# A fused four-layer model on one core: the third expert layer's order, VectorE splits, and a hand-written order in the last layer

## The chip, the cores and the metric

The kernel runs on one core of a Trainium2 chip. The metric is the device time of one execution in microseconds (us); the time before is the median of three runs. TensorE (PE in the profile) multiplies, VectorE (DVE), ScalarE (ACT) and GpSimd (POOL) do the element-wise work, and SyncE (SP) issues transfers.

## The reference, cut to what matters

Activations `x` of 4 batches x 512 tokens x 256 numbers go through eight steps, an attention and an expert layer in turn, each added to its input after a layer norm. All is float32.

```
x = x + L0_xattn(norm(x), ctx);  x = x + L0_ffn(norm(x))
x = x + L1_xattn(norm(x), ctx);  x = x + L1_ffn(norm(x))
x = x + L2_xattn(norm(x), ctx);  x = x + L2_ffn(norm(x))
x = x + L3_xattn(norm(x), ctx);  x = x + L3_ffn(norm(x))
```

The change touches three expert layers:

```
L0_ffn:  gates = softmax(x @ Wg); top 2, made to sum to 1
         out = sum over 8 experts e of weight[e] * (x @ We[e] + be[e])
L2_ffn:  shared = swiglu(x @ w_shared_in) @ w_shared_out
         hid = swiglu(x @ w1_shared)          # swiglu(a, b) = silu(a) * b
         out = shared + sum over 8 experts e of weight[e] * (hid @ w2[e])
L3_ffn:  scores = (relu(x @ W1 + b1) @ W2 + b2) * sigmoid(tanh(x @ Wg1 + bg1) @ Wg2 + bg2)
         e = argmax(softmax(scores));  out = x * scale[e] + bias[e]
```

## The kernel before, in words

The program is eight phases, numbered 0 to 7: attention in the even ones, experts in 1, 3, 5 and 7. Tokens are worked on in 4 batches of 4 tiles of 128. Every phase has one list of steps, `self.order`, and every engine walks that same list in order and issues its own part of each step. So a step's place in the list sets its place in the queue of every engine at once. In most phases the list comes from places on a number line: `spread(steps, begin, end)` gives steps evenly spaced places, and `in_order` sorts by them; a batch `g` has its main work at places `g` to `g + 1`. Within a step, semaphores order the engines. The results of TensorE go to the 8 PSUM banks in turn (`Ring`); a step that uses a bank waits until its last user has been emptied (`drained`). At a phase's start VectorE, ScalarE and GpSimd wait until all engines have left the phase before (`wait_left`); TensorE does not.

**Splits.** Products in phases 1, 3 and 5 need more precision than one pass gives: an operand is kept as `hi` (a rounded copy, made by ScalarE) and `lo` (the rest, a subtraction), and `mm3` multiplies hi by hi, hi by lo and lo by hi. In phases 1 and 5 the `lo` of the normed activations is made by GpSimd (`RowPairs.gpsimd`, L1205 to L1209), and the `lo` of the weights half by GpSimd, half by VectorE (`split_lo`, L1329 and L2334).

**Third expert layer** (`FeedForward2`, phase 5). A batch's first layer, the steps `f2_hidden`, multiplies 512 tokens by the two input weights in 4 steps of 12 matmuls of 512 columns. A step's two banks go through ScalarE (`silu`, L2324), VectorE (product, L2366), ScalarE (`hidden_hi`, L2329) and GpSimd (`hidden_lo`, L2409). Then each tile has one `f2_shared` step (6 matmuls of 256 columns; it waits for the last `hidden_lo`) and 4 `f2_routed` steps (6 of 512 each), which VectorE adds to `x` weighted (L2373, L2383). All 4 hidden steps stand at the head of the batch's list, in front of its own first tile.

**Last expert layer** (`FeedForward3`, phase 7). Batch 0 is worked on inside phase 6; 1 to 3 are left, and batch 3 has its layer norm still to come. Per batch: `f3_hidden` (two, relu and tanh), `f3_scores`, `f3_rows` (normed rows), `g_exp`, `g_div`, `g_top`, `g_places` (softmax and argmax on VectorE, `g_exp` on ScalarE), `f3_hot` (one-hot), `f3_turn` (transposed), and 4 `f3_row` (the chosen scale and bias rows by a matmul, times and plus on VectorE, the last sum on GpSimd). A batch is stored by one transfer when its four tiles are done.

Of the kernel before, what the change touches and what calls it, by code (L numbers as in the profile page):

```python
# [16 lines left out]
P = 128  # L17
# [5 lines left out]
KC = DM // P  # L23
# [204 lines left out]


def hT_read(c, f, b):  # L230

    def visited(step):
        k, v = c.at(step)
        return c.filled(k), v
    if f in (0, 4, 6):
        return [visited(("query", f, b, 1))]
    if f in (1, 5):
        return [visited(("logits", f, b)), (c.sem("h_lo"), c.nth["h_split", f, b])]
# [950 lines left out]
class RowPairs:  # L1189
# [14 lines left out]

    def gpsimd(self, e, step):  # L1205
        c, g = self.c, step[2]
        e.wait_ge(c.sem("h_hi"), c.nth[step])
        e.tensor_tensor(self[g].lo[:, :, :], c.hT[:, :, rows_of(g)], self[g].hi.bitcast(F32)[:, :, :],
                        ALU.subtract).then_inc(c.sem("h_lo"), 1)  # L1209

    def wait_made(self, e, g):
        e.wait_ge(self.c.sem("h_lo"), self.c.nth["h_split", self.f, g])


class FeedForward0:
# [53 lines left out]
    def tensor(self, e):  # L1269
        c, f, gates = self.c, self.f, self.gates  # L1270
        for step in self.order:
# [7 lines left out]
            elif kind == "f0_experts":  # L1279
# [5 lines left out]
                if t == 0:  # L1285
                    e.wait_ge(c.sem("f0_we_lo_pool"), e2 + 1)
                    e.wait_ge(c.sem("f0_we_lo_dve"), e2 + 1)
                if v > 1:
# [39 lines left out]

    def split_lo(self, e, k, sem):  # L1329

        c = self.c
        for e2 in range(E0 // 2):
            es = slice(2 * e2, 2 * e2 + 2)
            e.wait_ge(c.sem("f0_we_hi"), 2 * e2 + k + 1)
            e.tensor_tensor(self.we.lo[:, k, es, :], self.we_in[:, k, es, :], self.we.hi[:, k, es, :].bitcast(F32),  # L1335
                            ALU.subtract).then_inc(sem, 1)

    def vector(self, e):
        c, f, gates, norm = self.c, self.f, self.gates, self.norm
        for step in self.order:  # L1340
            kind = step[0]
            if kind == "f0_we":
                self.split_lo(e, 1, c.sem("f0_we_lo_dve"))
            elif kind == "logits":
# [47 lines left out]
    def gpsimd(self, e):  # L1392
        self.gates.make_iota(e)
        for step in self.order:
            if step[0] == "f0_we":
                self.split_lo(e, 0, self.c.sem("f0_we_lo_pool"))
            elif step[0] == "h_split":
                self.h.gpsimd(e, step)
            else:
                self.norm.gpsimd(e, step)  # L1400
# [785 lines left out]
class FeedForward2:  # L2186
# [28 lines left out]
    def work(self, sc, mine):  # L2215
# [8 lines left out]


        self.parts = [(name, k, slice(None)) for name in ("wsi", "w1", "wso") for k in range(KC)]
# [4 lines left out]
        for g in range(BATCH):  # L2231
# [20 lines left out]
    def wait_pair(self, e, name, e2=0):  # L2252

        c, n = self.c, {"wsi": 1, "w1": 2, "wso": 3, "w2": 4 + e2}[name]
        e.wait_ge(c.sem("f2_lo_pool"), n)
        e.wait_ge(c.sem("f2_lo_dve"), n)

# [75 lines left out]

    def split_lo(self, e, share, k, sem):  # L2334

        for n in self.shares[share]:
            name, q, part = self.parts[n]
            if q == k:
                e.wait_ge(self.c.sem("f2_hi"), n + 1)
                pair = self.pairs[name]  # L2340
                e.tensor_tensor(pair.lo[:, q, part], self.w[name][:, q, part], pair.hi[:, q, part].bitcast(F32),
                                ALU.subtract).then_inc(sem, 1)
# [53 lines left out]
    def gpsimd(self, e):  # L2396
        c, f = self.c, self.f
        self.gates.make_iota(e)
        for step in self.order:
            kind = step[0]  # L2400
            if kind == "f2_split":
                self.split_lo(e, step[2], 0, c.sem("f2_lo_pool"))
            elif kind == "h_split":
                self.h.gpsimd(e, step)
            elif kind == "f2_hidden":
# [12 lines left out]
class FeedForward3:  # L2418
# [76 lines left out]
    def work(self, sc, mine):  # L2495
# [170 lines left out]
class Phases:  # L2666
# [76 lines left out]
    def sync(self, e):  # L2743
        c = self.c
        for chain in CHAINS:
# [10 lines left out]
            for f in chain:  # L2756
                if f == 2:
                    self.wait_left(e, f)
                self.all[f].sync(e)
        for b in range(BATCH):  # L2760
            e.wait_ge(*x_final(c, LAST_PHASE, b))
            e.dma_start(c.out[b].rearrange("(t p) d -> p t d", p=P), c.x[:, 4 * b:4 * b + 4, :]).then_inc(c.sem(f"store{b}"), 16)
        for b in range(BATCH):
            e.wait_ge(c.sem(f"store{b}"), 16)

# [83 lines left out]
```

## Time and profile before

| what | value |
|---|---|
| median of 3 runs | 2894.68 us (2892.67 to 2896.89) |
| the profiled execution's own time | 2907.88 us |
| its span, first to last instruction | 2906.1 us |
| mean granted TensorE clock | 0.939 of full |
| TensorE busy | 2738.4 us, 94% |
| VectorE busy | 1632.2 us, 56% |
| ScalarE busy | 1579.1 us, 54% |
| GpSimd busy | 310.1 us, 11% |

Times in the trace are counted from the start of the span. Phase 1 begins at about 770 us, phase 5 at 1890 and phase 7 at 2853. In a row of the timeline the brackets say how long the engine had been idle before it and who released it. "PEclk" is the share of the full TensorE clock that was granted in a stretch: 1.00 is 2.4 GHz, 0.50 is 1.2 GHz. A busy TensorE that runs at 0.50 still counts as busy.

### The profile page before, as it was taken

To read this page: it belongs to the slowest core of one execution; us is meant where nothing else is said; L and a number is where in the kernel's file an instruction comes from. 1 tells how busy PE (TensorE), PEld (TensorE's weight loads), DVE (VectorE), ACT (ScalarE), POOL (GpSimd) and SP (SyncE) were. 2 spreads that over 40 slices of the span, in tenths; PEclk is the share of its full clock that TensorE was granted. 3 is DMA by queue.
4 is the path that set the end of the run, shared out by engine and by line. 5 is a ranking of instruction groups with operands and counts; after the bars stand their busy time and mean duration, and the time that the engine had idled before them with its cause. 6 is when DMAs were issued, how large, how long until landed. Compare 5 with 4: busy or idle time off the path is not lost.

```text
span 2906.1 us, 38394 instructions
## 1 busy us (share of the span) xinstructions
PE 2738.4 (94%) x14432; PEld 1356.7 (47%) x14432; DVE 1632.2 (56%) x2990; ACT 1579.1 (54%) x2687; POOL 310.1 (11%) x259
## 2 busy tenths in 40 slices
PE   7999999999899889999899999989999999999986
PEld 3334444343475557776333333368643443434333
DVE  6777777777375554442112221057576777777834
ACT  2777777777501112111687878831247777777762
POOL 2010100100111001211001010031301010010001
PEclk7899999999899999999999999989979998999977
DMA  5332243331200001001744545110133423324200
GB/s 120 62 45 42 40 53 51 46 34 13 88 1 29 1 15 51 1 1 43 108 56 68 76 56 62 44 48 1 29 47 50 57 47 46 56 32 50 24 1 29
DMA packets 68588, 125.13 MB, mean 43 GB/s; under 512 B 20963, under 2 KB 45102, under 8 KB 64950
## 3 DMA queue, kind: packets, MB, share of 16 engines
q1 hardware_dynamic: 67254, 120.25, 27.0%
q10 hardware_dynamic: 1152, 2.44, 0.3%
q8 instruction: 116, 1.90, 0.3%
q14 instruction: 66, 0.54, 0.1%
HBM read 42.11 MB, written 2.10 MB: 15 GB/s over the span
## 4 chain that ended last, share of the span: by engine, by line
PE 82%; DVE 9%; ACT 4%; issue 3%; SPq 2%; POOL 0%; DMA 0%; ACTq 0%; POOLq 0%; DVEq 0%
PE psum L190 53%; PE psum L726 19%; PE psum L1977 6%; DVE mpart L916 4%; ACT probs L794 3%; SPq L1032 1%; PE psum L279 1%; PE psum L736 1%; PE psum L1970 0%; SPq L1033 0%; DVE stats L306 0%; PE psum L745 0%; DVE parts L1798 0%; DVE hrow L331 0%; DVE we_pair_lo L1335 0%
## 5 line engine op out<-in xcount | busy, mean ns | idle before, releaser
L794 ACT ACTIVATE probs<-psum 128x512 f32<-128x512 f32 (+3 forms) x2080 | 1279.5, 693 | 403.2 <-PE psum L190 401.3
L916 DVE TENSOR_REDUCE mpart<-psum 128x2 f32<-128x804 f32 x1024 | 977.0, 991 | 323.1 <-PE psum L190 314.8
L726 PE MATMUL psum<-probs,vt 128*17 128x512 f32 (+1 forms) x4992 | 675.9, 617 | 1.4 <-ACT probs L794 1.4
L190 PE MATMUL psum<-qst,kst 50*128 50x512 f32 (+3 forms) x2496 | 615.0, 458 | 16.6 <-ACT probs L794 5.5
L190 PEld LDWEIGHTS psum<-qst,kst 50*128 50x128 f32 (+3 forms) x2496 | 273.6, 188 | 428.9 <-issue 270.0
L190 PE MATMUL psum<-kst,qst 48*128 48x402 f32 x2048 | 419.3, 435 | 39.3 <-DVE mpart L916 37.1
L190 PEld LDWEIGHTS psum<-kst,qst 48*128 48x128 f32 x2048 | 203.1, 201 | 347.9 <-issue 183.8
L190 PE MATMUL psum<-wv,ctxT 128*128 128x256 f32 (+1 forms) x624 | 185.3, 424 | 1.1 <-DVE vt L906 0.5
L726 PEld LDWEIGHTS psum<-probs,vt 128*17 128x17 f32 (+1 forms) x4992 | 85.0, 96 | 201.8 <-issue 161.3
L190 PE MATMUL psum<-ctxT,wk 128*128 128x512 f32 (+1 forms) x384 | 157.9, 541 | 9.5 <-DMA ctxT<-in_ctxT 8.0
L190 PEld LDWEIGHTS psum<-wv,ctxT 128*128 128x128 f32 (+1 forms) x624 | 110.2, 196 | 78.9 <-issue 59.9
L2022 ACT ACTIVATE inner<-psum 128x512 f32<-128x512 f32 x32 | 19.1, 597 | 214.6 <-PE psum L1977 214.6
L342 POOL TENSOR_TENSOR rstd<-veps,half 128x4 f32<-128x4 f32 x32 | 34.3, 1072 | 830.9 <-DVE veps L311 830.9
L989 POOL TENSOR_TENSOR kp_lo<-kp_lo,kp_hi 128x512 fp32r<-128x512 f32 x80 | 83.1, 1042 | 271.4 <-ACT kp_hi L783 205.1
L190 PEld LDWEIGHTS psum<-ctxT,wk 128*128 128x128 f32 x384 | 64.2, 193 | 89.9 <-issue 73.0
L906 DVE COPY vt<-psum 128x256 f32<-128x256 f32 (+1 forms) x52 | 22.1, 424 | 146.1 <-PE psum L190 146.1
L190 PE MATMUL psum<-we_pair_hi,masked_lo 128*128 128x512 f32 x256 | 88.1, 412 | 4.0 <-POOL we_pair_lo L1335 4.0
L1977 PE MATMUL psum<-masked_hi,w_hi 128*128 128x512 f32 x224 | 91.7, 409 | 0.0
L1977 PE MATMUL psum<-masked_hi,w_lo 128*128 128x512 f32 x224 | 89.4, 399 | 0.0
L1977 PE MATMUL psum<-masked_lo,w_hi 128*128 128x512 f32 x224 | 89.0, 397 | 0.0
L293 ACT ACTIVATE hT<-psum 128x512 f32<-128x512 f32 x56 | 32.9, 601 | 84.5 <-PE psum L279 84.4
L817 ACT ACTIVATE vt<-psum 128x256 f32<-128x256 f32 (+1 forms) x104 | 40.0, 392 | 63.9 <-PE psum L190 58.9
(325 smaller groups left out, 2710.7 us busy)
## 6 DMA issues: line engine op xcount, KB each, us to landing
kst<-kp_hi SPq DMA_DIRECT2D x144, 200.1 KB, 5.9
ctxT<-in_ctxT SPq DMA_DIRECT2D x36, 512.0 KB, 5.2
kst<-kp_lo SPq DMA_DIRECT2D x72, 200.1 KB, 5.4
qst<-qp_hi SPq DMA_DIRECT2D x144, 64.0 KB, 4.5
kst<-kp_hi SPq DMA_DIRECT2D x84, 100.1 KB, 2.9
qst<-qp_lo SPq DMA_DIRECT2D x72, 64.0 KB, 5.1
kst<-kp_lo SPq DMA_DIRECT2D x42, 100.1 KB, 3.0
stage<-in_L_ffn_W SPq DMA_DIRECT2D x16, 256.0 KB, 4.4
```

Of the source, the lines that this page charges most:

```text
L190: last = e.matmul(dst, lhsT, rhs, start=i == 0, stop=i == len(pairs) - 1)
L279: t = e.transpose(c.bank(k)[:, at:at + P], h[:, q * P:(q + 1) * P], c.ident[:, :])
L293: e.activation(dst, src, ACT.Copy).then_inc(c.drained(k), 1)
L342: e.tensor_tensor(c.rstd[:, ts], c.veps[:, ts], c.half[:, :], ALU.pow).then_inc(c.sem("rsqrt_made"), 1)
L726: t = e.matmul(c.bank(self.acc)[32 * h:32 * h + VW, :], self.vt[0:kn, kc, self.head(g, h), :], p[0:kn, h % self.wide, :], start=kc == 0, s ...
L736: t = e.transpose(bank[:, at], self.accs[:, at], c.ident[:, :])
L794: e.activation(self.probs[n % slots][0:kn, :, :], c.psum[0:kn, k:k + self.wide, :], ACT.Exp if softmax else ACT.Sigmoid, scale=DH ** -0.5) ...
L817: e.activation(dst, src, ACT.Copy).then_inc(c.drained(k), 1)
L916: e.tensor_reduce(self.mpart[:, :, p * (SEQ // P) + qt, i], c.psum[:, k:k + 2, 0:MAX_WIDTH], AX.X, ALU.max).then_inc(c.drained(k), 1)
L989: e.tensor_tensor(raw.bitcast(F32R), raw, hi.bitcast(F32), ALU.subtract).then_inc(c.sem("parts_made"), 1)
L1032: e.dma_start(ks.bitcast(F32)[rows, halves, :], k.bitcast(F32)[head, halves, :]).then_inc(sem, 16)
L1977: t = e.matmul(bank, *pair, start=i > 0 and j == 0, stop=j == len(passes) - 1)
```

## The change

1. **Splits.** The `lo` of the weights in phases 1 and 5, and of batch 0's activations in both, is made by VectorE alone. GpSimd keeps the activations of batches 1 to 3. Two semaphores of halves (`..._pool`, `..._dve`) become one.
2. **Third expert layer.** The 4 hidden steps of batches 1, 2 and 3 get the places `g - 0.26` to `g - 0.25`, inside the batch before them; batch 0's take 0 to 0.25 and its tiles 0.25 to 1.
3. **Last expert layer.** The order is written out. The last batch's norm comes early, and the adding of rows late.
4. **Last store.** Batch 3 is stored by two transfers of two tiles.

```diff
-    def gpsimd(self, e, step):
+    def low(self, e, step):
         c, g = self.c, step[2]
         e.wait_ge(c.sem("h_hi"), c.nth[step])
         e.tensor_tensor(self[g].lo[:, :, :], c.hT[:, :, rows_of(g)], self[g].hi.bitcast(F32)[:, :, :],
-                        ALU.subtract).then_inc(c.sem("h_lo"), 1)
+                        ALU.subtract).then_inc(low_rows_made(c, self.f, g)[0], 1)
...
             if kind == "f2_split":
-                self.split_lo(e, step[2], 1, c.sem("f2_lo_dve"))
+                self.split_lo(e, step[2])
+            elif kind == "h_split" and step[2] == 0:
+                self.h.low(e, step)
...
-            main = [("f2_hidden", f, g, which, i) for which in range(2) for i in range(KC)]
+            hidden = [("f2_hidden", f, g, which, i) for which in range(2) for i in range(KC)]
+            placed += spread(hidden, 0, 0.25) if g == 0 else spread(hidden, g - 0.26, g - 0.25)
+            main = []
...
-            placed += spread(ready, g - 0.9, g - 0.15) + spread(main, g, g + 1)
+            placed += spread(ready, g - 0.9, g - 0.15) + spread(main, g if g else 0.25, g + 1)
...
-        self.order = in_order(spread(self.batch_steps(1), -0.4, 0.15) + spread(self.norm.steps(f, 3), 0, 0.35)
-                              + spread(self.batch_steps(2), -0.1, 0.45) + spread(self.batch_steps(3), 0.37, 1))
+        self.order = hidden(1) + norm[:5] + hidden(2)[:1] + scores(1) + hidden(2)[1:] + norm[5:8] + rows(1) + norm[8:]
+        self.order += places(1) + scores(2) + hidden(3)[:1] + rows(2) + [("f3_turn", f, 1)] + hidden(3)[1:] + places(2)
+        self.order += [("f3_rows", f, 3)] + added(1) + scores(3) + [("g_exp", f, 3), ("f3_turn", f, 2)] + places(3) + added(2)
+        self.order += [("f3_turn", f, 3)] + added(3)
...
+            dst, size = c.out[b].rearrange("(t p) d -> p t d", p=P), 4 if b + 1 < BATCH else 2
+            for t in range(0, 4, size):
+                e.wait_ge(c.sem("f3_added"), c.nth["f3_row", LAST_PHASE, 4 * b + t + size - 1])
+                e.dma_start(dst[:, t:t + size, :], c.x[:, 4 * b + t:4 * b + t + size, :]).then_inc(c.sem(f"store{b}"), 16)
```

Here `places(g)` is `g_div`, `g_top`, `g_places`, `f3_hot`; `rows(g)` is `f3_rows`, `g_exp`; `added(g)` the four `f3_row`; and `norm` the last batch's norm without its idle place.

The first place is VectorE's queue at the start of phase 5, before (the `x` row is phase 4's last work, `w_202` is the routed part's input weight):

```order
L968 TENSOR_TENSOR x<-x,psum 128x256 x4
L2355 TENSOR_TENSOR gate_v<-psum,gb 128x32
L2341 TENSOR_TENSOR wsi_pair_lo<-wsi,wsi_pair_hi 128x512
L2341 TENSOR_TENSOR w_pair_lo<-w_202,w_pair_hi 128x512
L1121 TENSOR_REDUCE gate_m<-gate_v 128x4
```

and now:

```order
L975 TENSOR_TENSOR x<-x,psum 128x256 x4
L1216 TENSOR_TENSOR hpair_lo<-hT,hpair_hi 128x1024
L2364 TENSOR_TENSOR gate_v<-psum,gb 128x32
L2348 TENSOR_TENSOR wsi_pair_lo<-wsi,wsi_pair_hi 128x512 x2
L2348 TENSOR_TENSOR w_pair_lo<-w_202,w_pair_hi 128x512 x2
```

VectorE has gained the activations' `lo` and the second halves of both weights; GpSimd has lost them. Phase 1 begins in the same way.

The second place is VectorE's queue where batch 0 of phase 5 ends and batch 1 begins, before:

```order
L2373 TENSOR_TENSOR x<-x,psum 128x256
L2383 SCALAR_TENSOR_TENSOR x<-psum,gate_v,x 128x256 x8
L2366 TENSOR_TENSOR silu<-silu,psum 128x512 x3
L306 BN_STATS stats<-x 128x6
L308 BN_AGGR meanvar<-stats 128x2
L2366 TENSOR_TENSOR silu<-silu,psum 128x512
L2373 TENSOR_TENSOR x<-x,psum 128x256
```

and now:

```order
L2392 SCALAR_TENSOR_TENSOR x<-psum,gate_v,x 128x256 x4
L1155 TENSOR_TENSOR gate_hot<-iota,gate_idxf 128x32 x2
L2375 TENSOR_TENSOR silu<-silu,psum 128x512 x4
L2392 SCALAR_TENSOR_TENSOR x<-psum,gate_v,x 128x256 x4
L1167 TENSOR_TENSOR gate_hot<-gate_hot,gate_top_241 128x32 x2
L1169 TENSOR_TENSOR gate_v<-gate_hot 128x32
L2382 TENSOR_TENSOR x<-x,psum 128x256
L2392 SCALAR_TENSOR_TENSOR x<-psum,gate_v,x 128x256 x8
```

The four products of batch 1 (`silu`) now stand in the middle of batch 0's third tile, with half of that tile and the whole fourth behind them. Batches 2 and 3 have theirs in front of the fourth tile of the batch before. TensorE's queue is in the same order.

The third place is TensorE's queue in the last layer, before (`relu` and `tanh` mark the scores, `hrow` the last batch's norm, `hot` the transposed one-hot rows):

```order
L190 MATMUL psum<-hT,wg_218 128x512 x2
L190 MATMUL psum<-w_219,relu 128x16 x4
L2551 MATMUL psum<-ident,hot 48x128 x4
L190 MATMUL psum<-wg_220,tanh 128x1 x4
L190 MATMUL psum<-scale_bias,hotT 128x512 x4
L2551 MATMUL psum<-ident,hot 48x128 x4
L279 MATMUL psum<-ident,hrow 128x128 x8
L190 MATMUL psum<-scale_bias,hotT 128x512 x2
L190 MATMUL psum<-hT,w_217 128x512 x2
```

and now:

```order
L190 MATMUL psum<-hT,wg_218 128x512 x2
L286 MATMUL psum<-ident,hrow 128x128 x8
L190 MATMUL psum<-w_219,relu 128x16 x4
L190 MATMUL psum<-wg_220,tanh 128x1 x4
L190 MATMUL psum<-hT,w_217 128x512 x2
L2558 MATMUL psum<-ident,hot 48x128 x4
L190 MATMUL psum<-hT,wg_218 128x512 x2
L190 MATMUL psum<-scale_bias,hotT 128x512 x4
```

The norm's transposes, and with them batch 3's hidden steps, stand in front of all rows of scales and biases.

## Rows read from the trace of the kernel before

**Rows 1.** The page: its first line, and the chain that ended last, by engine

```profile
span 2906.1 us, 38394 instructions
...
PE 82%; DVE 9%; ACT 4%; issue 3%; SPq 2%; POOL 0%; DMA 0%; ACTq 0%; POOLq 0%; DVEq 0%
```

**Rows 2.** Timeline of TensorE, phase 5: start, us, engine, line, instruction, idle before

```profile
1895.61 0.76 PE L190 MATMUL psum<-hpair_hi,wsi_pair_hi 128*128 128x512 f32 x1 [3.82 <-POOL wsi_pair_lo L2341]
...
1915.21 0.55 PE L190 MATMUL psum<-wso_pair_hi,hidden_hi 128*128 128x256 f32 x1 [6.33 <-issue]
...
1916.63 3.42 PE L190 MATMUL psum<-wg,hT 128*128 128x8 f32 x16
...
1960.69 0.36 PE L190 MATMUL psum<-wso_pair_hi,hidden_hi 128*128 128x256 f32 x1 [3.73 <-issue]
...
2005.41 0.36 PE L190 MATMUL psum<-wso_pair_hi,hidden_hi 128*128 128x256 f32 x1 [2.96 <-issue]
...
2049.48 0.36 PE L190 MATMUL psum<-wso_pair_hi,hidden_hi 128*128 128x256 f32 x1 [2.96 <-issue]
```

**Rows 3.** Stretches of phase 5: length; PE, PEld, DVE, ACT, POOL busy; PEclk, DMA

```profile
1915.00:1924.00 9.00, 8.79 (x32) 7.95 (x33) 1.67 (x5) 0.34 (x1) 2.57 (x3) 0.50 0.00 0
1925.00:1946.00 21.00, 21.00 (x103) 17.68 (x102) 16.66 (x54) 0.23 (x1) 0.00 (x0) 1.00 0.00 1
1946.00:1960.00 14.00, 10.96 (x49) 8.75 (x47) 4.24 (x8) 8.20 (x11) 6.79 (x5) 1.00 0.00 1
1960.00:1972.00 12.00, 11.30 (x47) 9.90 (x48) 4.52 (x14) 0.23 (x1) 0.59 (x1) 0.72 0.00 0
2004.00:2012.00 8.00, 6.59 (x25) 5.47 (x26) 4.06 (x13) 0.00 (x0) 2.12 (x2) 0.79 0.01 3
```

**Rows 4.** Timeline of VectorE, GpSimd and TensorE at the start of phase 1

```profile
772.11 7.56 DVE L1335 TENSOR_TENSOR we_pair_lo<-we,we_pair_hi 128x512 fp32r<-128x512 f32 x4
...
774.03 6.78 POOL L1335 TENSOR_TENSOR we_pair_lo<-we,we_pair_hi 128x512 fp32r<-128x512 f32 x4
...
775.85 0.77 PE L190 MATMUL psum<-we_pair_hi,masked_lo 128*128 128x512 f32 x1 [3.98 <-POOL we_pair_lo L1335]
```

**Rows 5.** Timeline of VectorE, phase 5: a split while GpSimd is idle

```profile
1923.83 0.68 DVE L2341 TENSOR_TENSOR w_pair_lo<-w,w_pair_hi 128x512 fp32r<-128x512 f32 x1
```

**Rows 6.** Instructions of the tile hpair_lo: durations in ns, least, median, most

```profile
L2072 DVE TENSOR_TENSOR masked_lo<-hpair_lo,psum x16: 1210/1211/1215, 1087.6 to 1290.8; 128x1024 fp32r<-128x1024 f32 x16
```

**Rows 7.** Timeline of GpSimd and ScalarE, batch 0 of phase 5

```profile
1891.34 2.35 POOL L1208 TENSOR_TENSOR hpair_lo<-hT,hpair_hi 128x1024 fp32r<-128x1024 f32 x1 [0.50 <-ACT hpair_hi L1203]
...
1913.41 1.70 POOL L2409 TENSOR_TENSOR hidden_lo<-silu,hidden_hi 128x512 fp32r<-128x512 f32 x1
```

**Rows 8.** ScalarE in the same stretch

```profile
1911.33 0.63 ACT L2329 ACTIVATE hidden_hi<-silu 128x512 fp32r<-128x512 f32 x1 [0.75 <-DVE silu L2366]
```

**Rows 9.** Timeline of phase 7, all engines

```profile
2858.63 1.96 PE L190 MATMUL psum<-hT,w 128*128 128x512 f32 x4
...
2858.81 0.26 ACT L2582 ACTIVATE gate<-psum,minus_bg 128x4 f32<-128x4 f32 x1 [1.21 <-PE psum L190]
...
2859.73 1.38 DVE L2627 TENSOR_SCALAR h<-x,meanvar,rstd 128x256 f32<-128x256 f32 x4
...
2861.53 0.26 ACT L1113 ACTIVATE gate_v<-gate_v 128x64 f32<-128x64 f32 x1 [2.46 <-DVE gate_v L1123]
...
2863.91 0.36 DVE L2634 TENSOR_TENSOR hot<-places,gate_idxf 128x192 f32<-128x192 f32 x1
...
2877.18 0.73 DVE L331 TENSOR_SCALAR hrow<-x,meanvar,rstd 128x256 f32<-128x256 f32 x2
...
2878.24 1.05 PE L2551 MATMUL psum<-ident,hot 128*48 128x128 f32 x4 [10.79 <-DVE hot L2634]
...
2896.37 1.05 PE L2551 MATMUL psum<-ident,hot 128*48 128x128 f32 x4 [5.56 <-DVE hot L2634]
...
2899.89 2.77 POOL L2656 TENSOR_TENSOR x<-x,h 128x256 f32<-128x256 f32 x4 [9.29 <-DVE x L2643]
```

**Rows 10.** One stretch of phase 7, columns as in rows 3

```profile
2878.00:2907.00 29.00, 15.66 (x48) 8.54 (x48) 11.18 (x46) 4.27 (x8) 5.62 (x8) 0.62 0.11 36
```

**Rows 11.** The stores' transfers: count, KB each, us from issue to landing

```profile
out_dram<-x SPq DMA_DIRECT2D x3, 512.0 KB, 2.9
```

More of the change, by code:

```diff
@@ L227, in x_final, with low_rows_made @@
     return c.drained(k), v
+def low_rows_made(c, f, b):
+    nth = (1, 5).index(f)
+    return (c.sem("h_lo"), 3 * nth + b) if b else (c.sem("h_lo_first"), nth + 1)
 def hT_read(c, f, b):
@@ L237, in hT_read @@
     if f in (1, 5):
-        return [visited(("logits", f, b)), (c.sem("h_lo"), c.nth["h_split", f, b])]
+        return [visited(("logits", f, b)), low_rows_made(c, f, b)]
     if f == 2:
@@ L1327, in scalar, with split_lo @@
                 self.norm.scalar(e, step)
-    def split_lo(self, e, k, sem):
+    def split_lo(self, e):
         c = self.c
@@ L1333, in split_lo @@
             es = slice(2 * e2, 2 * e2 + 2)
-            e.wait_ge(c.sem("f0_we_hi"), 2 * e2 + k + 1)
-            e.tensor_tensor(self.we.lo[:, k, es, :], self.we_in[:, k, es, :], self.we.hi[:, k, es, :].bitcast(F32),
-                            ALU.subtract).then_inc(sem, 1)
+            for k in range(KC):
+                e.wait_ge(c.sem("f0_we_hi"), KC * e2 + k + 1)
+                e.tensor_tensor(self.we.lo[:, k, es, :], self.we_in[:, k, es, :], self.we.hi[:, k, es, :].bitcast(F32),
+                                ALU.subtract).then_inc(c.sem("f0_we_lo"), 1)
     def vector(self, e):
@@ L1394, in gpsimd @@
         for step in self.order:
[L1395 to L1398, printed above, removed]
+            if step[0] == "h_split" and step[2]:
+                self.h.low(e, step)
             else:
@@ L2332, in scalar, with split_lo @@
                 self.norm.scalar(e, step)
-    def split_lo(self, e, share, k, sem):
+    def split_lo(self, e, share):
         for n in self.shares[share]:
             name, q, part = self.parts[n]
[L2338 to L2342, printed above, removed]
+            e.wait_ge(self.c.sem("f2_hi"), n + 1)
+            pair = self.pairs[name]
+            e.tensor_tensor(pair.lo[:, q, part], self.w[name][:, q, part], pair.hi[:, q, part].bitcast(F32),
+                            ALU.subtract).then_inc(self.c.sem("f2_lo"), 1)
     def vector(self, e):
@@ L2348, in vector @@
             if kind == "f2_split":
-                self.split_lo(e, step[2], 1, c.sem("f2_lo_dve"))
+                self.split_lo(e, step[2])
+            elif kind == "h_split" and step[2] == 0:
+                self.h.low(e, step)
             elif kind == "logits":
@@ L2400, in gpsimd @@
             kind = step[0]
[L2401 to L2404, printed above, removed]
+            if kind == "h_split" and step[2]:
+                self.h.low(e, step)
             elif kind == "f2_hidden":
@@ L2500, in work, with hidden, scores, rows @@
                      for _ in range(3)]
-        self.order = in_order(spread(self.batch_steps(1), -0.4, 0.15) + spread(self.norm.steps(f, 3), 0, 0.35)
-                              + spread(self.batch_steps(2), -0.1, 0.45) + spread(self.batch_steps(3), 0.37, 1))
+        def hidden(g):
+            return [("f3_hidden", f, g, 0), ("f3_hidden", f, g, 1)]
+        def scores(g):
+            return [("f3_scores", f, g, 0), ("f3_scores", f, g, 1)]
+        def rows(g):
+            return [("f3_rows", f, g), ("g_exp", f, g)]
+        def places(g):
+            return [("g_div", f, g), ("g_top", f, g), ("g_places", f, g), ("f3_hot", f, g)]
+        def added(g):
+            return [("f3_row", f, t) for t in range(4 * g, 4 * g + 4)]
+        norm = [step for step in self.norm.steps(f, 3) if step[0] != "idle"]
+        self.order = hidden(1) + norm[:5] + hidden(2)[:1] + scores(1) + hidden(2)[1:] + norm[5:8] + rows(1) + norm[8:]
+        self.order += places(1) + scores(2) + hidden(3)[:1] + rows(2) + [("f3_turn", f, 1)] + hidden(3)[1:] + places(2)
+        self.order += [("f3_rows", f, 3)] + added(1) + scores(3) + [("g_exp", f, 3), ("f3_turn", f, 2)] + places(3) + added(2)
+        self.order += [("f3_turn", f, 3)] + added(3)
         ring = Ring(*range(8))
@@ L2760, in sync @@
         for b in range(BATCH):
-            e.wait_ge(*x_final(c, LAST_PHASE, b))
-            e.dma_start(c.out[b].rearrange("(t p) d -> p t d", p=P), c.x[:, 4 * b:4 * b + 4, :]).then_inc(c.sem(f"store{b}"), 16)
+            dst, size = c.out[b].rearrange("(t p) d -> p t d", p=P), 4 if b + 1 < BATCH else 2
+            for t in range(0, 4, size):
+                e.wait_ge(c.sem("f3_added"), c.nth["f3_row", LAST_PHASE, 4 * b + t + size - 1])
+                e.dma_start(dst[:, t:t + size, :], c.x[:, 4 * b + t:4 * b + t + size, :]).then_inc(c.sem(f"store{b}"), 16)
         for b in range(BATCH):
-            e.wait_ge(c.sem(f"store{b}"), 16)
+            e.wait_ge(c.sem(f"store{b}"), 16 if b + 1 < BATCH else 32)
     def wait_loaded(self, e, f):
```

11 lines of the change are left out of this document (4 added, 7 removed).

## The prediction

> **What bounds the kernel now.** I read the page's chain first: TensorE carries 82% of it and VectorE 9% [rows 1]. So the kernel is bound by TensorE's queue, and a change is worth what it takes from TensorE's idle time, from its time at the low clock, and from the last layer's chain, where TensorE is mostly not the bound. Next I read TensorE's timeline for idle time in the phases touched. In phase 5 it idles 3.82 us at the start and 6.33 us before batch 0's first tile, and 3.73, 2.96 and 2.96 us before the first tiles of batches 1 to 3 [rows 2]. These last come after the hidden steps, and each ends on `f2_shared`, which needs the last `hidden_lo`: product, `hidden_hi` and `hidden_lo` run while TensorE has nothing left to do. The stretches then show what idling costs afterwards: the clock was 0.50 in 1915 to 1924, 0.72 on the mean in 1960 to 1972 and 0.79 in 2004 to 2012, against 1.00 in 1925 to 1946, where TensorE never stopped [rows 3]. Last I followed phase 7: TensorE waits 10.79 us and then 5.56 us for one-hot rows from VectorE, since batch 3's norm is interleaved with the adding of batch 1's rows [rows 9], and its clock is 0.62 in that end [rows 10].
>
> The profiled execution took 2907.88 us, 1.8 us more than its span and 13.2 us more than the median of 2894.68 us. I make the sums against the trace and take the difference off the median; 13.2 us is 0.5%, so scaling a saving by it changes nothing here.
>
> **Part 1, splits in phase 1.** Before, TensorE starts at 775.85, released by GpSimd's first weight split [rows 4]. VectorE's four took 7.56 us and GpSimd's four 6.78 us side by side, 1.7 to 1.9 us each; one that ran while GpSimd was idle took 0.68 us [rows 4, 5]. After, VectorE makes the activations' `lo` and then eight splits. The trace has no 128x1024 subtraction from SBUF on VectorE; the nearest row, with one operand in PSUM, has 1.21 us [rows 6], and GpSimd's own takes 2.35 us [rows 7]. I take 1.21: from 772.2, 1.21 + 2 x 0.68 = 2.6 us gives 774.8, so **-1.1 us** (at 2.35 us it is 0). A step of TensorE uses two splits and takes 6.1 / 4.5 = 1.4 us at the full clock (a tile is four and a half such steps), twice that at the low one; VectorE makes two splits in 1.36 us, so there is no wait behind it, and the gates queued behind the splits start at 772.2 + 1.2 + 5.4 = 778.8 instead of 779.6.
>
> One rule speaks to this place. Rows 4 show both engines slow together, and rows 5 the short time. The Trainium skill, "SBUF — State Buffer", section "Who interferes with whom", says that a VectorE instruction with two SBUF inputs and a GpSimd instruction that reads SBUF shut each other out for their whole length. By that rule eight splits alone cost VectorE 5.4 us where two engines took 7; were 1.8 us VectorE's own price, it would be 14 us. The trace agrees with the rule, and the other reading is the third rival.
>
> **Part 2, batch 0 of phase 5.** Start: `lo` begins at 1891.34 as GpSimd's did [rows 7], then 1.21, 0.19 for the logits' copy (estimate, from the 128x32 operations beside it) and 2 x 0.68 give 1894.1 against 1895.61: 1.4 us earlier. Then the chain of the four hidden pieces ends the wait at 1915.21, not TensorE. In it GpSimd's last `hidden_lo` started at 1913.41 though its source was ready at 1911.96 [rows 7, 8], because other GpSimd work stood ahead: 1.45 us to gain. Against it, two splits (1.36 us) instead of one stand ahead of three of VectorE's products: up to +2.0 us, and more if GpSimd is in the way each time. I let these cancel and leave the tile at 1915.2. But batch 1's logits (3.42 us at the low clock) now stand in front of it, in the idle time, so the routed steps start 3.3 us sooner. They lose about 1.7 us of this, since the low clock of [rows 3] then holds for 3.3 us more of real work at half speed. With a share of the earlier start I take **-2.5 us**, between +1 (products late) and -5.8 (chain 2.4 us earlier as well).
>
> **Part 3, the three boundaries.** The hidden steps of batches 2 and 3 now have the preceding fourth tile behind them: 24 matmuls of 512 columns and 6 of 256; the 103 matmuls of 21 us [rows 3] are 3.4 such tiles, so 6.1 us each. Batch 1's have one and a half. The wait to be hidden is 3.73 us at most. All three go: 3.73 + 2.96 + 2.96 = 9.65 us. With them goes the low clock: (1 - 0.72) x 12 = 3.4 us, (1 - 0.79) x 8 = 1.7 us, and as much again at the third: 6.8 us. The sum is 16.4. What may be late next is VectorE: it is busy 16.66 of 21 us in the tiles and 4.24 of 14 us in the hidden steps [rows 3]. It gets no more work, only another mix, and the eight banks let it lag by several steps. I take **-16.0 us**; bounds -8 (half of the idle time stays, and part of the clock) and -17.
>
> **Part 4, the last layer.** TensorE starts as before, but batch 2's first hidden step (1.96 us) moves ahead of batch 1's scores, so the gate goes through ScalarE at 2858.81 + 1.96 = 2860.8 and VectorE goes on at 2861.1 [rows 9]. The last batch's statistics and GpSimd's root fit before that. From there VectorE's queue is the chain:
> - batch 1: gate 0.65, root 0.75, norm rows 1.46, normed rows 1.38, less the maximum 0.47, exponent 0.3, then 2.48 to the one-hot (2861.79 to 2864.27 in the rows): 7.5, to 2868.6
> - batch 2: scores 0.9, rows 1.38, maximum and exponent 0.77, one-hot 2.48: 5.5, to 2874.1
> - batch 3's rows 1.38 and batch 1's adding, 4 x 0.68 (GpSimd's four sums follow VectorE's pairs at 0.69 [rows 9]): to 2878.2
> - batch 3: scores 0.9, 0.77 and 2.48: to 2882.3; then batches 2 and 3 added, 5.4: to 2887.7
>
> Durations without a row of their own (0.65, 0.75, 0.47, 0.9) are small VectorE operations of 0.16 to 0.23 us, three or four in a row. TensorE's work between fits into these stretches at the full clock. GpSimd's last sum ends 0.7 later, at 2888.4, where before it ended at 2902.66. Between that and the span's end lie 3.4 us for the store; half the bytes at the end save part of 2.9 us [rows 11], between 0 and 1.4, and I take 0.8. The end comes at 2891.0, 15.1 us sooner. If TensorE's clock is low here as before, its matmuls of 1.9 us double on the way to the third one-hot, up to 2 us. I take **-14.4 us**, between -9 (one more queue turn of 5.5 us in VectorE's order) and -16.5.
>
> **Sum:** 1.1 + 2.5 + 16.0 + 14.4 = 34.0 us off, so 2894.7 - 34.0 = **2860.7 us**. All bounds together give -16 and -41: 2879 and 2854.
>
> **Rivals.**
> - *The low clock stays.* The idle time goes but the clock falls all the same, at other places, as it did after stretches that the change leaves alone. Then part 3 is 9.6 and part 2 is 1.0: -26.1, **2868.6**. Against it: the clock was 1.00 wherever TensorE did not stop [rows 3].
> - *The last layer gives half.* In a hand-written order one engine's wait holds everything behind it. Batch 3's root stands behind batch 1's scores in VectorE's queue, and its `hT` copy behind batch 1's exponent on ScalarE. If these chain up, 7.2 is lost: -26.8, **2867.9**.
> - *Splits cost 1.8 us each on VectorE.* Phase 1 then has 7 us more instead of 1.1 less (3.6 us of splits per step of 1.4 to 2.7), batch 0 of phase 5 about 8 more: +15 - 30.4, **2879**. Rows 5 speak against it.
> - *Slower: VectorE's queue becomes the bound at the boundaries.* The four products stand in its queue among tile sums and each waits for 12 matmuls. If VectorE were full in the tiles, the 9.8 us that it idles in each hidden stretch (14 less 4.24) would never be caught up once banks run out: 3 x 9.8 = 29 us more in place of 16 less, +29 - 18 = +11, **2906**. It decides from a busy share of 1 in the tiles; the row has 0.79.
> - *It does not do what it says.* `f2_shared` still ends on something late, such as `hpair_lo` or a bank, and the gaps move; with a last layer that keeps its length: about **2891**.
>
> **How the numbers follow.** Chances: forecast 0.65, low clock 0.12, half a last layer 0.10, dear splits 0.05, slower 0.04, nothing 0.04. A change of less than 0.2% (5.8 us) can't be told from none in this kernel. Faster is then 0.92, the same 0.04, slower 0.04. The range 2853 to 2876 takes in the first three cases and the bounds of the unknown costs but for their far corner.
>
> **What would show it.** In phase 5: no idle time above 1 us before `f2_shared` of batches 1 to 3, and a clock of 1.00 from 1930 on; batch 0's wait stays about 6 us with the logits in it. Phase 1: TensorE's first product at 774.8. Splits on VectorE near 0.68 us while GpSimd is idle. Phase 7: 38 us from its start to the span's end instead of 53, VectorE busy nearly throughout. I am wrong if TensorE waits for VectorE inside the tiles, if the clock falls in phase 5 without a gap, or if phase 7 still has a TensorE wait of 10 us.

## The result and the profile after

The changed kernel took 2851.27 us (median of 4 executions, 2849.18 to 2862.91) beside 2894.87 us for the kernel before (4 executions, 2892.67 to 2896.89): a ratio of 0.9855 with a 95% interval of 0.9826 to 0.9883. The forecast was 2860.7 with a range from 2853 to 2876, so the sign was right and the time lies 1.7 us below the range. The profiled execution took 2849.68 us, 1.8 us more than its span; the one of before took 2907.88. Two later executions of the kernel before took 4751 us and are, as slow ones, in no ratio and no mean.

First the chain and the head of the page of the kernel after. TensorE carries the same 82% of a shorter span, and the idle time called "issue" is 2% instead of 3% [rows 1]:

```profile
span 2847.9 us, 38377 instructions
...
PE 82%; DVE 9%; ACT 4%; issue 2%; SPq 2%; DMA 0%; ACTq 0%; POOL 0%; POOLq 0%; DVEq 0%
```

Next TensorE's timeline in phase 5 of the kernel after, the same columns as [rows 2]:

```profile
1883.98 0.47 PE L190 MATMUL psum<-hpair_hi,wsi_pair_hi 128*128 128x512 f32 x1 [2.27 <-DVE wsi_pair_lo L2348]
...
1896.60 1.85 PE L190 MATMUL psum<-wg,hT 128*128 128x8 f32 x16
1904.16 0.55 PE L190 MATMUL psum<-wso_pair_hi,hidden_hi 128*128 128x256 f32 x1 [5.71 <-issue]
...
1993.33 0.66 PE L286 MATMUL psum<-ident,hrow 128*128 128x128 f32 x4 [1.93 <-DVE hrow L338]
```

The start wait is 2.27 us (3.82 before); batch 0's wait is 5.71 us (6.33), and batch 1's logits stand in front of it. The waits of 3.73, 2.96 and 2.96 us have no row left. A new one has come: 1.93 us before a turn, for rows that VectorE norms for the next layer. The clock, in long stretches of the same phase (columns as in [rows 3]):

```profile
1904.00:1944.00 40.00, 39.84 (x180) 33.53 (x181) 24.93 (x66) 9.60 (x13) 7.59 (x6) 0.94 0.00 1
1944.00:1984.00 40.00, 40.00 (x201) 33.93 (x200) 27.07 (x85) 7.29 (x12) 6.16 (x5) 1.00 0.00 1
1984.00:2024.00 40.00, 38.07 (x188) 31.98 (x187) 29.23 (x93) 10.82 (x16) 9.55 (x7) 0.96 0.00 1
2024.00:2048.30 24.30, 24.30 (x122) 20.49 (x121) 19.35 (x52) 1.20 (x2) 1.01 (x1) 1.00 0.00 1
```

The granted clock is 1.00 in the second and the fourth stretch. In the first it is low right behind batch 0's wait, in the third behind the new wait; a stretch of 8 us cut as in [rows 3] around the latter shows 0.79, as behind the second boundary of the kernel before:

```profile
1993.00:2001.00 8.00, 7.67 (x41) 6.74 (x42) 6.17 (x19) 3.54 (x4) 2.93 (x2) 0.79 0.00 1
```

The kernel before had, in three stretches of 40 us from its 1915.6 on:

```profile
1915.60:1955.60 40.00, 40.00 (x179) 34.00 (x179) 22.54 (x66) 4.98 (x8) 4.55 (x4) 0.89 0.00 1
1955.60:1995.60 40.00, 36.27 (x170) 30.59 (x169) 23.70 (x77) 6.76 (x10) 5.82 (x4) 0.91 0.00 0
1995.60:2035.60 40.00, 37.04 (x184) 30.98 (x183) 29.74 (x96) 9.04 (x14) 9.54 (x7) 0.96 0.01 1
```

Phase 7 of the kernel after, TensorE, VectorE and GpSimd. In place of the waits of 10.79 and 5.56 us of [rows 9] TensorE has one wait of 4.05 us and none other above 0.8 us:

```profile
2810.58 1.99 PE L190 MATMUL psum<-hT,w 128*128 128x512 f32 x4 [0.51 <-DVE x L975]
...
2824.91 0.36 DVE L2655 TENSOR_TENSOR hot<-places,gate_idxf 128x192 f32<-128x192 f32 x1
...
2836.98 2.04 PE L190 MATMUL psum<-scale_bias,hotT 48*128 48x512 f32 x4 [4.05 <-ACT hotT L2611]
...
2843.97 0.41 DVE L2664 TENSOR_TENSOR x<-x,psum 128x256 f32<-128x256 f32 x1
...
2839.58 5.66 POOL L2677 TENSOR_TENSOR x<-x,h 128x256 f32<-128x256 f32 x8 [4.11 <-DVE x L2664]
```

The last layer takes 37.3 us from its first matmul to the span's end (2810.58 to 2847.9), against 52.9 before (2853.18 to 2906.1).

**Where the 43.6 us went.** Three marks fix the touched code in any trace: the products of phase 1 (from the start of its first matmul of `we_pair_hi` by `masked_lo` to the start of the last), the products of phase 5 (from the start of the first matmul of `wsi_pair_hi` to the start of the last of `w_pair_hi` by `hidden_hi`), and the time from phase 7's first ReLU to the end of the span. All the rest is the same code in both kernels, but for the two starts. From one trace to the other the products of phase 1 give 0.6 us, those of phase 5 16.2, the end 15.6, the two starts 1.2 and 1.5: 35.1 us. The forecast's sum was 34.0. The attention between phase 5 and phase 7, the same code in both, took 779.2 us before and 764.4 after: 14.8 us that no term speaks of. Was that chance, or a gain that follows from the change? The medians differ by 43.6 us, 8 more than the marks.

### The profile page after: what moved, and what is told of

Read it like the earlier page. It is cut to its first block, busy times and chain, and to the rows that moved or that the text cites. A ratio compares the mean times of both kernels' runs of the same rounds, so it can differ in the third digit from the quotient of the medians.

```text
span 2847.9 us, 38377 instructions
## 1 busy us (share of the span) xinstructions
PE 2704.7 (95%) x14432; PEld 1338.9 (47%) x14432; DVE 1634.5 (57%) x3003; ACT 1577.6 (55%) x2687; POOL 289.1 (10%) x246
## 4 chain that ended last, share of the span: by engine, by line
PE 82%; DVE 9%; ACT 4%; issue 2%; SPq 2%; DMA 0%; ACTq 0%; POOL 0%; POOLq 0%; DVEq 0%
PE psum L190 53%; PE psum L733 20%; PE psum L1985 6%; DVE mpart L923 5%; ACT probs L801 3%; SPq L1039 1%; PE psum L286 1%; PE psum L743 1%; PE psum L1978 1%; SPq L1040 0%; DVE stats L313 0%; PE psum L752 0%; DVE hrow L338 0%; DVE parts L1806 0%; SPq L617 0%
## 5 line engine op out<-in xcount | busy, mean ns | idle before, releaser
L190 PE MATMUL psum<-qst,kst 50*128 50x512 f32 (+3 forms) x2496 | 610.2, 454 | 16.2 <-ACT probs L801 5.1
L948 DVE COPY ctxn<-psum 128x512 f32<-128x512 f32 x16 | 11.0, 688 | 108.7 <-PE psum L733 108.7
```

Of the source, the lines that this page charges most:

```text
L190: last = e.matmul(dst, lhsT, rhs, start=i == 0, stop=i == len(pairs) - 1)
```

## The experiments

The times of a row are those of one profiled execution; its ratio is of 4 to 12 executions. "Layer" is phase 5's products, "end" is phase 7 from its first ReLU, "attention" lies between them, and "rest" is the span without the products of phases 1 and 5 and without the end, the attention included. Ratios are to the kernel before in the same measurement. Some rows share one measurement and its executions of before (`again3`, `again4` and `best2` do), so their ratios are not independent.

| run | layer | end | attention | rest | ratio (95% interval) |
|---|---|---|---|---|---|
| before | 180.5 | 50.8 | 779.2 | 2558.7 | |
| before_again | 181.4 | 50.8 | 772.9 | 2550.1 | |
| after (first result) | 164.3 | 35.2 | 764.4 | 2533.0 | 0.9855 (0.9826 to 0.9883) |
| again | 165.4 | 35.4 | 757.9 | 2538.8 | 0.9878 (0.9841 to 0.9914) |
| again2 | 164.3 | 35.3 | 771.0 | 2558.1 | 0.9859 (0.9820 to 0.9898) |
| again3 | 164.2 | 35.4 | 770.7 | 2549.1 | 0.9864 (0.9830 to 0.9898) |
| again4 | 165.5 | 35.3 | 768.2 | 2538.3 | 0.9864 (0.9831 to 0.9897) |
| no_hidden | 181.1 | 35.6 | 780.3 | 2561.7 | 0.9938 (0.9914 to 0.9962) |
| no_last | 165.2 | 52.7 | 767.7 | 2538.6 | 0.9927 (0.9902 to 0.9953) |
| no_split | 164.1 | 35.2 | 774.5 | 2561.3 | 0.9875 (0.9837 to 0.9914) |
| hidden_only | 165.3 | 52.7 | 771.5 | 2555.4 | 0.9952 (0.9926 to 0.9977) |
| last_only | 180.2 | 35.4 | 764.8 | 2557.8 | 0.9959 (0.9935 to 0.9982) |
| short_cover | 170.8 | 35.5 | 769.7 | 2547.8 | 0.9884 (0.9850 to 0.9918) |
| late_w2 | 162.7 | 35.5 | 774.7 | 2545.3 | 0.9854 (0.9822 to 0.9885) |
| one_store | 164.3 | 36.1 | 770.9 | 2541.2 | one execution |
| best | 162.8 | 34.6 | 771.4 | 2553.4 | 0.9861 (0.9825 to 0.9897) |
| best2 | 161.5 | 32.7 | 774.5 | 2546.3 | 0.9848 (0.9815 to 0.9880) |

### Chance or a follow-on: the kernels unchanged

> The changed kernel as it is, a second time. Open after the first result: the medians differ by 43.6 us, while the stretches of code that the change touches differ by only some 35 us between the two profiled executions (first layer's start -1.2 and products -0.7, third layer's start -1.5 and products -16.2, last layer -15.6), and stretches with the same code in both (the attention of the layer before the last above all, 779.2 us before and 764.4 after) make up the rest or more. Theory A (the rest is chance: where dips of TensorE's granted clock fall in unchanged attention code from one execution to the next): the attention stretch before the last layer comes out anywhere between 764 and 779 us here, the touched stretches within 1 us of the first trace, and the ratio to before moves by several us from the first one, 34 to 44 us less than before. Rival B (the changed third layer makes the attention behind it faster): that stretch is 764 +- 2 us again, and the gain is 43 +- 2 us again.

Measured: 2859.63 us, a ratio of 0.9878, 35 us below before. The touched stretches came out within 1.1 us of the first trace, but the attention took 757.9 us, less than either theory had named.

> The changed kernel a third time. Eight executions with the change's parts in several combinations show the touched stretches fixed to within 1.2 us each (third layer's products 164.1 to 165.4 where they were moved, end 35.2 to 35.6 with the hand-written order), while the stretches with the same code in all of them add up to anything from 2533 to 2562 us; the trace that the first result came with had the least of all, 2533. Theory A (chance in the unchanged code): the touched stretches again 35 us below before together, the unchanged ones 2538 to 2562, and a gain nearer to the second measurement (35 us) than to the first (42 to 44). Rival B (the unchanged code is truly faster behind the change): the unchanged stretches at 2533 to 2540 again and a gain of 42 us or more.

> The kernel before, a second trace. Theory A: third layer's products 180.5 +- 0.7 us and end 50.8 to 52.7, while the unchanged stretches differ from the first trace's 2559 by up to 15 us either way. Rival B: they are within 3 us of it.

> The changed kernel a fourth time, for the size of the gain alone. Three measurements gave 0.9855, 0.9878 and 0.9859 of before (42, 35 and 41 us), each with an interval of some 10 us either way, while the touched stretches give 34.4 and the attention behind the third layer 0.8: 35.2 us, a ratio of 0.9878. Theory A: the ratios scatter about 0.987 to 0.988 and the stretches with the same code add up to 2533 to 2562 us. Rival B: they stay at 0.985 to 0.986, and there is a gain of 5 us or more that the marks do not show.

> The same as the run before it, once more on the same chip: by A the two medians may differ by 5 us from each other though the kernel is the same; by B they agree within 2 us.

Measured: 2860.78, 2857.15 and 2860.89 us, and before 2898.77 in its one execution. The rest of the kernel after went from 2533.0 to 2558.1 us over five traces of the same program, 25 us, and that of before came out 8.6 us less than the first time. The attention as a whole, from the layer's last product to the first ReLU, of `again`, `again2` and `no_hidden` (columns as in [rows 3]):

```profile
2062.00:2819.90 757.90, 721.83 (x4141) 298.91 (x4140) 542.15 (x744) 521.38 (x1015) 66.92 (x61) 0.96 0.31 43
2067.10:2838.10 771.00, 735.07 (x4141) 305.52 (x4140) 542.22 (x744) 521.79 (x1015) 66.79 (x61) 0.93 0.31 42
2078.20:2858.50 780.30, 745.85 (x4141) 309.33 (x4140) 542.83 (x745) 522.07 (x1015) 66.92 (x61) 0.91 0.30 41
```

VectorE, ScalarE and GpSimd do the same work in the same time, and TensorE sends the same 4141 matmuls; what differs is the granted clock, and with it TensorE's busy time. It is so in all 17 traces: 757.9 us at a clock of 0.96; 764.4 to 768.2 at 0.94; 769.7 to 774.7 at 0.93; 779.2 at 0.92; 780.3 at 0.91. So most of the 14.8 us was a draw of the clock (A), and the first trace of after had the least rest of all 17. B keeps a small part. In the kernels without the full cover (before twice, no_hidden, last_only, short_cover) the first matmul of the attention that reads `accs` comes 50.5 to 50.7 us behind the layer's last product, in the other twelve 49.4 to 49.9. That is 0.8 us. The whole attention took 773.4 us on the mean of these five traces and 769.8 on the mean of the twelve. The difference of 3.6 us is less than the scatter within either kind (764.8 to 780.3 and 757.9 to 774.7), so whether B is worth more than the 0.8 us is not shown. The stretches of after and before from 20 to 40 us behind the layer, with a clock of 0.69 and 0.55:

```profile
2068.30:2088.30 20.00, 15.77 (x56) 8.06 (x55) 18.23 (x20) 1.69 (x5) 6.91 (x5) 0.69 0.89 119
```

```profile
2096.10:2116.10 20.00, 17.14 (x54) 9.07 (x54) 17.34 (x19) 1.85 (x6) 7.06 (x5) 0.55 0.87 119
```

The marks then give 34.4 (below) and 0.8, 35.2 us in all. The five ratios have a mean of 0.9864, which is 39 us. Each interval holds 0.988, the ratio of 35 us. Taken together the executions say more: 27 of after have a mean of 2859.9 us (standard deviation 7.5), 70 of before 2898.8 (8.6). That is 38.8 us, with an error of some 3.5 either way (estimate from these deviations), so 35.2 us lies at the edge. `again3` and `again4` do not decide it: their 0.9864 lies between what A and B had named, and their medians differ by 3.7 us, which goes with A. Whether the 4 us left are real stays open.

### Each part taken out, and each alone

```
no_hidden:   main = [("f2_hidden", f, g, which, i) ...]          # in their own batch again
             placed += ... + spread(main, g, g + 1)
no_last:     self.order = in_order(spread(self.batch_steps(1), -0.4, 0.15) + ...)
             e.dma_start(c.out[b]..., c.x[:, 4 * b:4 * b + 4, :])  # one piece
no_split:    low parts of weights and of h shared by VectorE and GpSimd as before
hidden_only: before, with "hidden" spread over g - 0.26 to g - 0.25
last_only:   before, with the hand-written order and the two-piece store
```

> The changed kernel with the third layer's first products back inside their own batch. My theory (9.65 us of idle time at three batch boundaries and 6.8 us of low clock behind them, worked out as 16.0, and part of batch 0's start with it): 16 us above the changed kernel, waits of 2.9 to 3.8 us back before the first shared product of batches 1 to 3 and the granted clock under 1.00 behind them. Rival 'the clock does not come back': only the idle time, 9 to 10 us. Rival B (the attention behind the third layer gains by the fuller third layer): 16 us in the layer and some 10 to 15 more in the attention behind it, 26 to 31 us in all, with that attention at 775 to 780 us.

> The kernel before with one part alone: the third layer's first products a fourth of a batch earlier. By the forecast's terms: 16.0 in the three boundaries and 1 to 2 of batch 0's 2.5, 17 to 18 us below before, with the stretch from the third layer's first to its last product at 164 to 165 us. Open is the attention behind that layer: over five executions it took 779 and 780 us where the products were in their own batch, and 758, 764, 768 and 775 us where they were moved. Chance (A): this and the other runs of the moved products fall anywhere from 758 to 781. Follow-on (B): the attention behind stays below 776 here, and the kernel is 22 to 30 us below before.

`no_hidden` puts the three waits back, in TensorE's timeline:

```profile
1962.79 0.36 PE L190 MATMUL psum<-wso_pair_hi,hidden_hi 128*128 128x256 f32 x1 [3.74 <-issue]
...
2007.50 0.35 PE L190 MATMUL psum<-wso_pair_hi,hidden_hi 128*128 128x256 f32 x1 [2.96 <-issue]
```

The layer is at 181.1 us, 16.4 above the mean of after's five traces (164.7); `hidden_only` is at 165.3, 15.7 below the mean of before's two. Of the idle time, 9.66 us, the new wait for `hrow` takes 1.93 back, which leaves 7.7; so about half of the gain came from the clock and from batch 0, whose wait is shorter and has the logits in front of it. In time, 0.9938 against 0.9864 is 21 us, and `hidden_only` is 14 us below before: 18 on the mean. The follow-on of 10 to 15 us that B wanted is not there: the attention took 771.5 us in `hidden_only`.

> The changed kernel with the last layer's order made by the spreading rule again and batch 3's store in one piece. My theory: 14 to 16 us above the changed kernel, all of it behind the last layer's first ReLU (51 us instead of 35). Rival 'half': 7 to 8 us, if the hand order gains only what the store in two pieces and the last batch's chain give. The attention before the last layer has nothing to do with it: 764 to 779 us by chance (A), or 764 by B.

> The kernel before with the other part alone: last layer in the hand-written order and batch 3's store in two pieces. By the forecast's terms: 14 to 16 us below before, all behind the last layer's first ReLU (35.2 instead of 50.8 us). The attention before the last layer stands behind the old third layer here: by B it takes 777 to 782 us, by A anything from 758 to 781.

The end took 52.7 and 35.4 us. In time `no_last` is 18 us above the changed kernel (0.9927 against 0.9864) and `last_only` 12 us below before. `last_only`'s attention of 764.8 us stands behind the old third layer and decides against B as it was written, which had 777 to 782. A surprise was the end of 52.7 us with the old order in `no_last` and in `hidden_only`, against 50.8 in both traces of before. One row tells it, of `hidden_only` and then of before_again: the same four matmuls, at the low clock and mostly at the full one.

```profile
2867.91 3.78 PE L190 MATMUL psum<-hT,wg 128*128 128x512 f32 x4
```

```profile
2877.42 2.00 PE L190 MATMUL psum<-hT,wg 128*128 128x512 f32 x4
```

So the last layer's part is worth 15.5 us where the clock rose at that place before, and 17.4 where it did not. Both traces with 52.7 us have the old order behind the new third layer, both with 50.8 us stand behind the old one. Whether the third layer's change shifts the clock there, or chance does, two traces of a kind do not show.

> The changed kernel with the low parts of the splits shared between VectorE and GpSimd as before. My theory: the two layers' starts lose 1.1 us (first layer, its first low part) and up to 2.5 us (third layer's start), 1.2 to 3.6 us above the changed kernel. Rival 'dear splits' (VectorE's subtractions at 1.7 to 2.6 us each beside a working GpSimd make batch 0's wait of 5.7 us in the third layer): 2 to 4 us below the changed kernel, and that wait under 3 us.

The two starts lose 1.2 us (a wait of 3.98 against 2.77 in phase 1) and 1.55 us (3.82 against 2.27 in phase 5), 2.8 together, inside the 1.2 to 3.6 expected; the layer's products take 164.1. In time it is 0.9875 against 0.9864, which is less than can be told. The rows of the changed kernel, on VectorE with eight splits and with two, and then a pair beside GpSimd:

```profile
765.18 4.90 DVE L1343 TENSOR_TENSOR we_pair_lo<-we,we_pair_hi 128x512 fp32r<-128x512 f32 x8
...
1881.31 1.23 DVE L1216 TENSOR_TENSOR hpair_lo<-hT,hpair_hi 128x1024 fp32r<-128x1024 f32 x1 [1.32 <-ACT hpair_hi L1210]
1882.55 1.29 DVE L2348 TENSOR_TENSOR wsi_pair_lo<-wsi,wsi_pair_hi 128x512 fp32r<-128x512 f32 x2
...
1898.90 2.55 DVE L2348 TENSOR_TENSOR w_pair_lo<-w,w_pair_hi 128x512 fp32r<-128x512 f32 x2 [1.22 <-ACT w_pair_hi L2322]
...
1899.18 1.72 POOL L2416 TENSOR_TENSOR hidden_lo<-silu,hidden_hi 128x512 fp32r<-128x512 f32 x1
```

In a row a split takes 0.61 to 0.65 us, beside GpSimd's `hidden_lo` 1.27. The trace agrees with the rule of the Trainium skill that the prediction cites ("SBUF — State Buffer", section "Who interferes with whom"); the sums of the touched stretches go by the rows alone.

### How much cover is needed, and what bounds batch 0

```
short_cover: placed += ... spread(hidden, g - 0.05, g - 0.04)
late_w2:     f2_split shares at (-0.95, 0.05, 0.11, 0.251, 0.252)
```

> The changed kernel with only the last routed step of the preceding batch behind the products that were moved, instead of a whole tile. A routed step is 1.4 us at the full clock and the waits to be hidden are 3.73, 2.96 and 2.96 us. Forecast: waits of about 2.3, 1.6 and 1.6 us are back, 5.5 us, and the low clock behind them with part of its 6.8 us: 5.5 to 11 us above the changed kernel's 164.3 us in the layer's products. Rival 'one step is enough' (the wait is only for the last piece, and the logits and others fill in): under 2 us.

The waits are back at 1.54, 1.60 and 1.60 us, 4.7 instead of the 5.5 forecast, and the layer is 6.1 us longer than after's mean. The low clock did not come back with them: cut as in [rows 3], the stretches from the first and the second wait on show 1.00, where the kernel before had 0.72 and 0.79. Of the 1.4 us left, some 0.5 us stand ahead of the waits, since batch 0's tile came 21.1 us behind the first product (20.5 on the mean of after's five traces); where the rest arises is open.

```profile
1954.55 0.35 PE L190 MATMUL psum<-wso_pair_hi,hidden_hi 128*128 128x256 f32 x1 [1.54 <-issue]
...
1994.69 0.36 PE L190 MATMUL psum<-wso_pair_hi,hidden_hi 128*128 128x256 f32 x1 [1.60 <-issue]
...
1954.00:1966.00 12.00, 11.45 (x64) 10.07 (x65) 7.63 (x23) 1.56 (x3) 2.81 (x2) 1.00 0.00 0
1994.00:2002.00 8.00, 7.31 (x38) 6.34 (x39) 5.19 (x16) 0.00 (x0) 0.59 (x1) 1.00 0.01 2
```

> The changed kernel with the splits of the third layer's second weights behind the hidden pieces of batch 0 instead of between them. In the trace of the changed kernel TensorE waits 5.71 us for the last hidden_lo, and VectorE spends 1.96, 2.55 and 1.95 us on pairs of splits between the products, each pair behind 1.1 to 1.2 us in which it waits for ScalarE. Theory (those splits make the wait): the first shared tile of batch 0 comes 2 to 3 us earlier; 1 to 2 us of it are lost again at the first routed step, which then waits for the two late splits; the layer's products take 0 to 2 us less than 164.3. Rival (GpSimd's and ScalarE's own pieces make the wait): the tile is no earlier, and the layer takes 1 to 3 us longer.

The wait fell from 5.71 to 3.08 us, the tile came 1.5 us or more earlier (18.7 us behind the first product, against 20.2 to 21.1 in after's five traces), and the layer takes 162.7 us, 2.0 less than after's mean. The splits between the pieces made part of the wait.

```profile
1904.96 0.55 PE L190 MATMUL psum<-wso_pair_hi,hidden_hi 128*128 128x256 f32 x1 [3.08 <-issue]
```

### The end, and better versions

```
one_store: one dma_start of 512 KB for batch 3
best:      late_w2, and ("f3_rows", f, 1), ("f3_rows", f, 2) ahead of scores(1)
best2:     best, and rows(2) (batch 2's exponent) ahead of hidden(3)[:1]
```

> The changed kernel with batch 3's result stored in one piece of 512 KB. In the forecast the two pieces were worth 0.8 us, between 0 and 1.4: the time from GpSimd's last sum to the span's end should be 3.4 us here against 2.7, and the stretch from the last layer's first ReLU to the end 36.0 instead of 35.2 to 35.6. Rival (the end is a fixed delay of a transfer): no difference.

The end is 36.1 us, 0.8 more than after's mean of 35.3, as the forecast had it; this rests on one execution, and after's five ends lie between 35.2 and 35.4.

> The changed kernel with the late splits of the run before and, in the last layer, the normed rows of batches 1 and 2 ahead of batch 1's scores in VectorE's queue. VectorE idles 3.55 us there in the changed kernel's trace and is the bound of all that follows; the two groups of four take 1.37 and 1.38 us. Theory: 2.0 to 2.7 us off the end (32.7 to 33.4 us instead of 35.4), with 1.6 to 2 us from the splits 4 us below the changed kernel, about 39 us below before. Rival (TensorE's queue or GpSimd's sums take over): under 1 us off the end.

Only 0.7 us came off the end. The 2.7 us of normed rows did move into VectorE's idle time, but then VectorE waited for batch 2's exponent, which stood on ScalarE behind a ReLU whose product TensorE made at the low clock:

```profile
2846.00 0.22 DVE L1133 TENSOR_REDUCE gate_m<-gate_v 128x4 f32<-128x64 f32 x1 [2.38 <-ACT gate_v L1120]
```

> The kernel of the best version with one more step: batch 2's exponent ahead of batch 3's first product in the last layer. In the trace of the best version ScalarE ran the ReLU behind that product first (TensorE took 3.54 us for it at the low clock), and VectorE waited 2.38 us for the exponent. Theory: 1.6 to 2.1 us off the end (32.5 to 33.0 us instead of 34.6). Rival (TensorE's one-hot rows of batch 1 come next and hold VectorE): under 0.7 us.

With the exponent ahead, the wait is 0.32 us and the end 32.7 us:

```profile
2836.15 0.22 DVE L1133 TENSOR_REDUCE gate_m<-gate_v 128x4 f32<-128x64 f32 x1 [0.32 <-ACT gate_v L1120]
```

By the marks this version is 5.0 us below the changed kernel: 2.4 in the layer (`late_w2`, `best` and `best2`, with the same code there, had 162.3 on the mean) and 2.6 at the end. By time it has 0.9848 against 0.9864 twice in the same measurement: 4.6 us, in the same direction but inside the intervals.

## Why the prediction was right and where it was wrong

- **Part 1, -1.1 us:** 1.2 us, from the waits. The 0.6 us that phase 1's products gave in the first pair of traces is not counted: they took 116.0 and 114.7 us in the two traces of before and 115.5 to 115.7 in the five of after. The splits took 0.61 us each and `masked_lo` 1.22 (taken: 0.68 and 1.21). The third rival, splits at 1.8 us each, is out.
- **Part 2, -2.5 us:** the start gave 1.5 us. The forecast said 1.4, though its own terms (1895.61 less 1894.1) give 1.5. The logits stand in front of the wait. The tile came 20.2 to 21.1 us behind the first product, against 19.6 and 20.0 before: the two effects that I let cancel left some 0.7 us of loss, and `late_w2` shows the splits in it.
- **Part 3, -16.0 us:** the layer's products, with part 2's remainder (1.1 us), 17.1 forecast and 16.2 measured (mean of two traces of before less mean of five of after). All three waits went, and the clock was 1.00 behind them. What I had not counted is the wait of 1.93 us for `hrow` and the low clock behind it, so the sign "a clock of 1.00 from 1930 on" did not come true; VectorE as the bound of the tiles (the slower rival) was not seen.
- **Part 4, -14.4 us:** 15.5. The chain stood up link by link. From TensorE's first matmul, the one-hot rows of batch 1 were forecast after 15.4 us and ended after 14.7, VectorE's last addition after 34.5 and 33.8, the span's end after 37.8 and 37.3. The 0.7 us arose in the first link and stayed to within 0.2. "The last layer gives half" is out.
- **Sum:** 34.0 forecast, 34.4 by the marks (1.2, 1.5, 16.2 and 15.5), and 0.8 behind the third layer.

**The step that failed** is the one from the sum to the range: "All bounds together give -16 and -41: 2879 and 2854". The range holds the unknowns of the change alone, and the paragraph on the profiled execution treats the rest as a constant ("13.2 us is 0.5%, so scaling a saving by it changes nothing here"). It is not one. The code outside the change takes 2533 to 2562 us, in attention by the clock that TensorE is granted there, and a median of four executions carries part of that. The first result drew a fast one: with a standard deviation of 7.5 us between executions, a median of four scatters by some 4 us (estimate), and 2851.27 lies 8.6 us below the mean of all 27. Four later medians of the same kernel were 2857.15 to 2860.89 us, inside the range and within 4 us of 2860.7. That closeness holds some luck too: the kernel before had means of 2899.3 to 2900.3 us beside them, 5 to 6 us above the 2894.7 from which the forecast was taken off. As a gain, 34.0 us was forecast and 38.8 is the mean of all executions. So of the 9.4 us by which the result missed the forecast, about half was the draw, and about half is a gain short by some 5 us, of which the marks show 0.4 and the attention's start 0.8. The spread was in view: the profiled execution lay 13 us above the median of its own kernel. What stays open is whether the other 4 us are real.

## What to carry to other kernels

Before naming a range, find out how much the code that a change does not touch varies between executions, and add it to the bounds of the change. Judge a small part by marks inside the trace, where it stood within 1.3 us over five traces here, and not by medians, which moved by 9.6 us for one and the same program. When an order is written by hand, follow the last link on every engine: the gain of `best` was held by one exponent queued behind a ReLU on ScalarE.

## What the runs showed of the hardware

- Over 17 traces, code that is the same in all of them took 2533 to 2562 us. Its longest stretch, the attention behind the third expert layer, took 757.9 us at a mean granted clock of 0.96 and 780.3 us at 0.91, with the same number of matmuls; two traces of one program (`again`, `again2`) had 0.96 and 0.93. What sets the clock apart in them is open.
- Waits of 1.54 and 1.60 us at a boundary left the clock at 1.00 in the 12 and 8 us from them on, while in the kernel before, after waits of 3.73 and 2.96 us, it fell to 0.72 and 0.79 in stretches of the same length [rows 3]. A wait of 1.93 us elsewhere in the changed layer was followed by 0.79 over 8 us.
- A VectorE split of 128x512 takes 0.61 us in a row of eight, 1.27 us beside a GpSimd subtraction of the same size, which took 1.72 us.
